# A macaron block on one core: router logits with the router as stationary operand, a new written-out order, and idle matmuls placed inside it

## What is computed

```python
x = x + 0.5 * ffn(layernorm(x))
x = x + attn(layernorm(x))          # 16 heads of 16, each query sees the last 64 keys
x = x + 0.5 * ffn(layernorm(x))

def ffn(X):                         # E = 8 routed experts, top K = 2, and a shared one; hidden 128
    shared = silu(X @ sW1 + sb1) @ sW2 + sb2
    logits = X @ routing_W.T + expert_bias
    activation = sqrt(softplus(logits))
    top_vals, top_idx = top_k(activation, 2)
    combine = sum(one_hot(top_idx, 8) * top_vals[..., None], axis=-2)
    y = silu(X @ rW1[e] + rb1[e]) @ rW2[e] + rb2[e]      # for every expert e
    return shared + einsum('ne,end->nd', combine, y)
```

## Time and profile before

| | us |
|---|---|
| median of 3 runs | 1542.52 (1542.23 to 1547.29) |
| profiled execution | 1542.9 |
| its span, first to last instruction | 1541.2 |
| PE busy in the span | 1496.8 (97%) |
| DVE, ACT, POOL busy | 1160.1, 1132.4, 803.4 |
| mean granted TensorE clock | 0.987 |

### The profile page before, as it was taken

How to read it: one execution, slowest core, us unless ns; L and a number is a source line. 1 busy time by engine, 2 the same in 40 slices (tenths; PEclk the granted TensorE clock), 3 DMA queues, 4 the chain that set the end, 5 groups by cost and what they waited for, 6 DMA issues and landing times.

```text
span 1541.2 us, 41196 instructions
## 1 busy us (share of the span) xinstructions
PE 1496.8 (97%) x13863; PEld 1350.0 (88%) x13863; DVE 1160.1 (75%) x4773; ACT 1132.4 (73%) x3416; POOL 803.4 (52%) x794
## 2 busy tenths in 40 slices
PE   8988999999999999999999999999999999999898
PEld 7887889888998889899898988989898898989787
DVE  6767777868788686877868788786877778686664
ACT  6467777778777777777778777777867778677753
POOL 4444555546455554645546465554645556354443
PEclk9999999999999999999999999999999999999799
DMA  3165536364363635536263453727335362534410
GB/s 119 39 183 149 156 103 194 83 179 132 95 174 111 186 98 152 145 101 183 97 173 119 130 140 117 193 76 193 118 113 156 121 176 84 161 101 133 119 54 28
DMA packets 264391, 199.65 MB, mean 130 GB/s; under 512 B 150859, under 2 KB 220918, under 8 KB 264182
## 3 DMA queue, kind: packets, MB, share of 16 engines
q1 hardware_dynamic: 263972, 196.94, 44.7%
q10 hardware_dynamic: 178, 0.02, 0.0%
q0 software_dynamic: 32, 0.07, 0.0%
HBM read 141.86 MB, written 42.43 MB: 120 GB/s over the span
## 4 chain that ended last, share of the span: by engine, by line
PE 73%; DVE 10%; issue 5%; SPq 4%; POOL 4%; DMA 2%; ACT 2%; DVEq 0%; POOLq 0%; ACTq 0%
PE gb L1069 10%; PE gb L1071 10%; PE gb L1070 9%; PE yb L1069 7%; PE yb L1070 7%; PE yb L1071 7%; PE ptb L1142 6%; PE sb_ L1133 5%; PE cxb L1161 3%; POOL gl L676 2%; PE gb L1183 2%; PE gb L1181 2%; DMA gate<-gates_pair 2%; DVE pr L938 2%; SPq L583 2%
## 5 line engine op out<-in xcount | busy, mean ns | idle before, releaser
L676 POOL TENSOR_TENSOR gl<-ag,gh 128x512 fp32r<-128x512 f32 x288 | 387.9, 1352 | 310.6 <-ACT gh L779 306.6
L732 ACT ACTIVATE pr<-pr,mx 128x128 f32<-128x128 f32 x1024 | 397.2, 392 | 35.1 <-DVE mx L938 31.5
L659 POOL TENSOR_TENSOR pr<-pr,rinv 128x512 f32<-128x512 f32 x256 | 278.3, 1094 | 233.2 <-DVE rinv L946 231.7
L1069 PE MATMUL yb<-w2h,gh 128*128 128x256 f32 x1152 | 334.9, 291 | 3.6 <-POOL gl L676 3.3
L1071 PE MATMUL yb<-w2l,gh 128*128 128x256 f32 x1152 | 322.6, 280 | 0.0
L1070 PE MATMUL yb<-w2h,gl 128*128 128x256 f32 x1152 | 322.5, 280 | 0.0
L938 DVE CUSTOM_DVE_ANT_0 pr<-sb_,mask 128x128 f32<-128x128 f32 x1024 | 236.0, 286 | 76.0 <-PE ptb L1142 48.8
L794 ACT ACTIVATE tt<-gb,b1half 128x512 f32<-128x512 f32 x288 | 195.9, 682 | 122.8 <-PE gb L1071 109.2
L1069 PE MATMUL gb<-xh,w1h 128*128 128x512 f32 x576 | 243.1, 422 | 2.3 <-DVE ag L1010 1.8
L779 ACT ACTIVATE gh<-ag 128x512 fp32r<-128x512 f32 x288 | 178.7, 626 | 83.6 <-DVE ag L1016 50.0
L1010 DVE SCALAR_TENSOR_TENSOR ag<-gb,b,gate 128x512 f32<-128x512 f32 x256 | 188.8, 745 | 65.7 <-ACT tt L794 33.4
(11 more groups left out here) (157 smaller groups left out, 2776.1 us busy)
## 6 DMA issues: line engine op xcount, KB each, us to landing
gate<-gates_pair SPq DMA_DIRECT2D x240, 256.0 KB, 3.9
ks<-qk_dram SPq DMA_DIRECT2D x256, 128.0 KB, 2.8
qs<-qk_dram SPq DMA_DIRECT2D x512, 64.0 KB, 2.5
...
```

Of the source, the lines that this page charges most:

```text
L659: nc.gpsimd.tensor_tensor(pr[:, k], pr[:, k], rinv[:, k, :].unsqueeze(2).to_broadcast([P, NP, P]), ALU.mult).then_inc(a_pn, 1)
L676: nc.gpsimd.tensor_tensor(gl[:, k, :], ag[:, k, :], gh[:, k, :].bitcast(F32), ALU.subtract).then_inc(f_gl, 1)
L732: nc.scalar.activation(pr[:, k, r, :], pr[:, k, r, :], ACT.Exp, bias=mx[:, k, r:r + 1], scale=-1.0, accum_out=rsum[:, k, r:r + 1]).then_in ...
L1069: nc.tensor.matmul(dst, ah, bh, start=start, stop=False, **kw)
```

## The change

**Logits.** The router becomes the stationary operand, padded with zeros to 128 columns (`rw` grows). `L` is four matmuls of 512 columns (two halves of the features, `xh` and `xl`), which give rounded-part logits on rows 0 to 7 and residue logits on rows 8 to 15. ACT copies the 128x512 result to SBUF (new step `lt`), and PE's new step `M` multiplies it, in four plain f32 matmuls of 8 columns, with a 0/1 matrix `fold` that both turns it back and adds the two parts. DVE then needs one addition where it had two.

**Constants.** POOL makes `fold` (a memset, two selects) and zeroes the pad of `rw` (a memset): `NCONST` goes from 19 to 23.

**Order.** All tables are written anew. New `Zg` steps are idle matmuls that write into the bank of the next step that takes one (so they wait for that bank). `ORDER` has two of them with two matmuls each (ahead of `P0` and of `pY1`, 36 matmuls in nine rounds), `HEAD` has 23, `TAIL` 60. Plain `Z` matmuls are 81 in `HEAD` and 16 in `TAIL`.

**Waits.** Three are added that the tables' order already implies (`aR` for `qT`, both halves of `ST` for the write of the scores' operands, the first experts' `a` for the weights' residues).

```diff
-qY8-7 S1-5 U15-6 V1-5 pY0-4 S2-5 O0-6 P0-5 S3-5 pH1-4 P1-5 S4-5 pH2-4 O1-6 S5-5 pH3-4 U1-5 pH4-4 pY1-4 P2-5
+V1-5 S1-5 qY8-7 S2-5 Zg2:P0-5 P0-5 pY0-4 O0-6 S3-5 O1-6 pH1-4 pH2-4 S4-5 pH3-4 pH4-4 P1-5 Zg2:pY1-4 pY1-4
+qX0-6 P2-5 U1-5 S5-5 qX1-6 pY2-4 P3-5 pH5-4 S6-5 qL-6 pH6-4 S7-5 pY3-4 qM-6 pY4-4 P4-5 U3-5 pY5-4 P5-5 pH7-4
...
-        rw = sb("rw", [P, KC, 2 * E], F32R)
+        rw = sb("rw", [P, KC, P], F32R)
+        fold = sb("fold", [P, E])
...
+            nc.gpsimd.memset(fold[:], 0.0).then_inc(w_const, 1)
+            nc.gpsimd.memset(rw[:, :, 2 * E:].bitcast(F32), 0.0).then_inc(w_const, 1)
...
+            select(fold[:], ALU.not_equal, 1.0, 0, [[-1, E]], 1)
+            select(fold[:], ALU.not_equal, 1.0, -E, [[-1, E]], 1)
...
+                elif s[1:] == "lt":
+                    n = nth(s, b)
+                    act.wait_ge(f_lgt, n + 1)
+                    nc.scalar.activation(lgt, bank(s[0] + "L", b), ACT.Copy).then_inc(f_lgs, 1)
...
-                acc = psum[:, 0:NT * 2 * E].rearrange("p (t e) -> p t e", t=NT)
-                op(nc.vector.tensor_tensor(lg[:], acc[:, :, E:2 * E], ebias[:].unsqueeze(1).to_broadcast([P, NT, E]),
-                                           ALU.add))
-                op(nc.vector.tensor_tensor(lg[:], acc[:, :, 0:E], lg[:], ALU.add))
+                op(nc.vector.tensor_tensor(lg[:], psum[:, 0:NT * E].rearrange("p (t e) -> p t e", t=NT),
+                                           ebias[:].unsqueeze(1).to_broadcast([P, NT, E]), ALU.add))
...
+                if s[:2] == "Zg":
+                    tile = take_bank(*users[next(ahead)])
+                    for _ in range(int(s[2:].split(":")[0])):
+                        nc.tensor.matmul(tile[:, 0:P], ident[:], ident[:], start=True, stop=True, skip_group_check=True)
...
-                    for t in range(NT):
-                        ts = slice(t * P, (t + 1) * P)
-                        for k in range(KC):
-                            nc.tensor.matmul(tile[:, 2 * E * t:2 * E * t + 2 * E], xh[:, q, k, ts], rw[:, k, :],
-                                             start=(k == 0), stop=False, skip_group_check=True)
-                            mm = nc.tensor.matmul(tile[:, 2 * E * t:2 * E * t + E], xl[:, q, k, ts], rw[:, k, 0:E],
-                                                  start=False, stop=(k == KC - 1), skip_group_check=True)
+                    for k in range(KC):
+                        nc.tensor.matmul(tile, rw[:, k, :], xh[:, q, k, :], start=(k == 0), stop=False)
+                        mm = nc.tensor.matmul(tile, rw[:, k, :], xl[:, q, k, :], start=False, stop=(k == KC - 1))
+                    mm.then_inc(f_lgt, 1)
+                elif s[1] == "M":
+                    n = nth(s, b)
+                    pe.wait_ge(f_lgs, n + 1)
+                    for t in range(NT):
+                        mm = nc.tensor.matmul(bank(s[0] + "L", b)[:, E * t:E * t + E], lgt[:, t * P:(t + 1) * P], fold[:],
+                                              start=True, stop=True, skip_group_check=True)
```

More of the change, by code:

```diff
@@ new lines @@
+pH6=1 P1=0 pH7=1 Z2=0 S4=0 pH8=1 P2=0 S5=0 pX0=2 U1=0 pX1=2 P3=0 S6=0 S7=0 pY6=1 P4=0 U3=0 pL=2 P5=0 S8=0
+pY7=1 P6=0 S9=0 pY8=1 P7=0 U5=0 S10=0 pM=2 pH0=2 U7=0 P8=0 Zg2=0 S11=0 Zg5=0 P9=0 Zg4=0 S12=0 aX0=1 P10=0
+aX1=1 U9=0 S13=0 Zg2=1 Q00=1 P11=0 Q01=1 S14=0 pC=2 U11=0 P12=0 S15=0 V0=1 Q10=1 Q11=1 P13=0 pY0=2 pH1=2
+U13=0 P14=0 pH2=2 pH3=2 P15=0 pH4=2 U15=0 pY1=2 V1=1 S0=1 O0=0 O1=0 S1=1 pY2=2 pY3=2 S2=1 pH5=2 S3=1 pH6=2
+P0=1 pH7=2 pY4=2 P1=1 S4=1 qX0=0 qX1=0 U1=1 P2=1 S5=1 pY5=2 qL=0 P3=1 S6=1 pH8=2 qM=0 qH0=0 U3=1 S7=1 P4=1
@@ new lines @@
+pH4=12 S5=11 qX0=10 P3=11 S6=11 pY1=12 qX1=10 pY2=12 pH5=12 S7=11 pH6=12 qL=10 pY3=12 qM=10 pY4=12 U3=11
+P4=11 pY5=12 pH7=12 pH8=12 qH0=10 P5=11 pY6=12 S8=11 P6=11 U5=11 qC=10 S9=11 pY7=12 P7=11 S10=11 pY8=12
+qH1=10 qH2=10 pX0=13 S11=11 U7=11 qY0=10 P8=11 qH3=10 pX1=13 qH4=10 qY1=10 P9=11 aX0=12 qY2=10 aX1=12 qH5=10
+qH6=10 P10=11 S12=11 pL=13 qY3=10 P11=11 Q00=12 pM=13 S13=11 U9=11 U11=11 qY4=10 S14=11 Q01=12 qH7=10 qH8=10
+P12=11 qY5=10 pH0=13 qY6=10 Q10=12 S15=11 V0=12 P13=11 qY7=10 qY8=10 U13=11 pC=13 P14=11 Q11=12 P15=11
@@ new lines @@
+pY0=13 U15=11 S0=12 V1=12 S1=12 Zg3=12 S2=12 O0=11 O1=11 P0=12 S3=12 pH1=13 P1=12 pH2=13 S4=12 pH3=13 U1=12
+P2=12 S5=12 pH4=13 S6=12 qX0=11 P3=12 pY1=13 qX1=11 S7=12 pY2=13 pH5=13 pH6=13 qL=11 pY3=13 qM=11 pY4=13
+U3=12 P4=12 pY5=13 pH7=13 P5=12 pH8=13 qH0=11 S8=12 P6=12 U5=12 pY6=13 qC=11 S9=12 pY7=13 P7=12 S10=12
+pY8=13 qH1=11 qH2=11 pX0=14 S11=12 U7=12 qY0=11 pX1=14 P8=12 qH3=11 qH4=11 qY1=11 P9=12 aX0=13 aX1=13 qY2=11
+P10=12 S12=12 qH5=11 P11=12 qY3=11 pL=14 Q00=13 S13=12 pM=14 U9=12 U11=12 qY4=11 Q01=13 S14=12 qH6=11 qH7=11
@@ new lines @@
+qH8=11 qY5=11 S15=12 P12=12 Q10=13 qY6=11 V0=13 P13=12 pC=14 Q11=13 U13=12 P14=12 pH0=14 qY7=11 P15=12
+qY8=11 S0=13 U15=12 V1=13 pY0=14 S1=13 O0=12 O1=12 S2=13 P0=13 Zg2=13 P1=13 pH1=14 S3=13 pH2=14 pH3=14 S4=13
+U1=13 P2=13 pH4=14 S5=13 P3=13 qX0=12 S6=13 pY1=14 pY2=14 qX1=12 S7=13 pH5=14 pH6=14 qL=12 pY3=14 qM=12
+pY4=14 U3=13 P4=13 pY5=14 pH7=14 pY6=14 pH8=14 qH0=12 P5=13 S8=13 qC=12 U5=13 P6=13 pY7=14 P7=13 S9=13
+qH1=12 pY8=14 S10=13 pX0=15 qH2=12 U7=13 qH3=12 qY0=12 S11=13 P8=13 qH4=12 pX1=15 S12=13 qY1=12 aX0=14 P9=13
@@ new lines @@
+qY2=12 aX1=14 qH5=12 S13=13 qY3=12 pL=15 P10=13 Q00=14 pM=15 P11=13 qY4=12 Q01=14 qH6=12 S14=13 qH7=12 U9=13
+U11=13 qY5=12 Q10=14 qH8=12 S15=13 qY6=12 pH0=15 P12=13 Q11=14 qY7=12 P13=13 pC=15 V0=14 qY8=12 P14=13
+U13=13 S0=14 P15=13 pY0=15 S1=14 U15=13 V1=14 S2=14 O0=13 P0=14 S3=14 O1=13 pH1=15 pH2=15 P1=14 S4=14 pH3=15
+P2=14 S5=14 pH4=15 U1=14 qX0=13 S6=14 P3=14 pY1=15 qX1=13 pY2=15 pH5=15 pH6=15 qL=13 pY3=15 qM=13 S7=14
+pY4=15 P4=14 pY5=15 pH7=15 P5=14 pH8=15 qH0=13 P6=14 pY6=15 S8=14 U3=14 U5=14 qC=13 S9=14 pY7=15 P7=14
@@ L459, in run @@
                 for s, off in words(ORDER[engine]):
-                    if 0 <= i + off < B and (s, i + off) not in apart_:
+                    if 0 <= i + off < B and (s[s.find(":") + 1:], i + off) not in apart_:
                         step(s, i + off)
@@ L500, in macaron_block @@
         run("PE", note)
+        ahead = iter(ahead)
         def bank(s, b):
```

382 lines of the change are left out of this document (183 added, 199 removed).

## The result

| | before | after |
|---|---|---|
| median | 1542.4 us (1538.3 to 1547.3, 4 runs) | 1619.1 us (1616.0 to 1624.9, 4 runs) |
| profiled span | 1541.2 | 1614.3 |
| mean granted clock | 0.987 | 0.987 |

The change makes the kernel 5% slower: ratio 1.050 (1.047 to 1.052). The forecast was 1541 us, in a range of 1527 to 1556.

The account below looks back on a forecast made before the run. PE was taken as the bound, with free time in head and tail. Logits +4.5, rounds +2, head 0 and tail -8 gave -1.5 us on the 1541.2 span, stated as 1541 us, range 1527 to 1556.

Parts of the forecast that it names:

- What bounds the kernel: Whole kernel: PE is the bound, 1496.8 of 1541.2 us busy; free time is in the head and above all the tail.
- Idle matmuls in the round: Repeating rounds: idles at P0 and pY1 partly fill waits; 0.9 us of planned waits replace 0.97 at C.
- The term for all rounds: Nine repeating rounds: waits and idle matmuls together cost +2 us, between -3 and +9.
- The logits on PE: L, M and an edge between unlike matmuls: 1.84 us against 1.70 a pass, +4.5 us in 32 passes.
- the doubt on f32: At M: if each of four FP32 passes needed its own load, 1.7 us, adding 27 us in all.
- rival 4: At L: long matmuls reusing weights overlap more, 0.13 us each, -12 us in all, 1529; chance 0.02.
- The logits elsewhere: ACT's copy adds 18.8 us, DVE loses 6.1; in the rounds costed at nothing, about 2 us where the router's result is awaited.
- The head: Before the rounds: first X up to 0.8 us later, against 20.8 us of PE idle time; 0, from -6 to +4.
- The tail: Last batches: idle matmuls keep the clock up and expert work moves behind the last O; -8 us, at best 13 gained.
- Rival 2: Each round and three like it in the tail gain a 1 us wait, at M or P0 and pY1; 1553; chance 0.19.
- rival 1: No new waits replace the old: rounds -3, head -6, tail -13, logits +3; 1524, or 1530; chance 0.28.
- Rival 3: In the tail the clock falls despite idles, or attention's chain sets the end: tail 0, 1549; chance 0.11.

Follow-up runs that it names:

- e2: Changed kernel with two SyncE steps, VS and OUT, moved behind the first four gate loads in all its tables: 1580.4 us, ratio 1.024.
- e5: e2 with the old logits (sixteen short matmuls at L; lt and M do nothing): 1586.5 us, ratio 1.032.
- e12: Changed kernel's new logits in every engine's order of the kernel before, without idle matmuls: 1652.6 us, ratio 1.073.
- e15: e12 with only lt and M put earlier, in the repeated rounds and the tail: 1604.7 us, ratio 1.040.
- e14: Changed code in the order of the kernel before, with the old logits and no idle matmuls: 1553.0 us, ratio 1.007.
- e8: Kernel before with 32 idle matmuls put into PE's waits in the attention of batch 15: 1538.8 us, ratio 0.9987.
- e4: Changed kernel with all 119 Zg idle matmuls left out: 1626.2 us, ratio 1.053.

## Why the prediction was wrong

**What bounds the kernel.** Right in that PE is the bound and that what it waits for is what counts. But it reads nothing of SyncE's queue. The step that failed is this one, under "Idle matmuls in the round": "So the new order has by its own plan 0.9 us of waits a round in exchange for the 0.97 at `C`." The term for all rounds was +2, with +9 as its upper end; the nine rounds measured +44.1, and the stretch up to the last attention, for which the sum has no term of its own, +18.8. The step looked at PE's table alone, at two places where idle matmuls had been put. SyncE's table was not costed at all, though the change puts `QW1` (1 MB) ahead of `pG1`, and `VS` (768 KB) ahead of the gates' loads. The trace of before could have shown the danger: DVE already waited 1.37 us for the gates in that round, and `H3` started 0.05 us behind the step that freed its bank. The price of `VS` and `OUT` ahead of the loads is 39 us (e2).

**The rounds without that.** e2's rounds are still 1.7 us longer than 91.2. The places: 0.54 ahead of `P0` and 0.94 ahead of `pY1`, the idles in them included; 0.42 ahead of `pY0`; 0.2 ahead of `pY2`; 0.54 ahead of the `S` behind `C`; two passes of the logits 0.2; less the 0.97 at the old `C`: 1.9 us, a little more than the 1.7. The trade was a loss, as the term of +2 had it, but its size was wrong: waits and idles of 2.7 us a round stand against the 0.97, and not 0.9. The longer way to the gates (`L`, `lt`, `M`) is not what costs here: with the old logits in the same order the rounds are no shorter (e5, 93.7), and the gates of `p` are copied earlier than before (those of `q`, counted from `S0`, 1.3 us later in e2). It costs where the order was not made for it (e12 to e15). How much of the new order's waits was needed to make room for it was not shown.

**The logits on PE.** Right, and a little dear. Rows of one pass, the start of `L` and of `M`, each with what stands behind it:

```profile
1563.41 0.39 PE L1205 MATMUL gb<-xh,rw 128*128 128x512 f32 x1
...
1564.34 0.39 PE L1089 MATMUL gb<-xh,w1h 128*128 128x512 f32 x1
...
1565.74 0.95 PE L1212 MATMUL gb<-fold,xn 128*128 128x8 f32 x8
1566.55 0.48 PE L1089 MATMUL gb<-xh,w1h 128*128 128x512 f32 x1
```

Here `L` is 0.93 us (forecast 0.91) and `M` 0.81 (0.85), together 1.74 where the old `L` took 1.70. That is the shortest of both. Over all 32 passes `L` takes 0.98 us on average and `M` 0.85, together 1.83, 0.09 more than the shortest, about the edge that was forecast at 0.08. The old `L` took 1.70 us in one kind of pass and 1.79 in the other, where a `P` follows it, on average 1.75 without one pass that stood in a wait. So it is +0.08 us a pass, +2.6 us in all, where the sum had +4.5. (By the prediction's own bounds the term's upper end is +5.4 us, not +7.) `M` stands as eight records for four matmuls, and costs 0.81 us and not 1.7, so the doubt on f32 fell as foreseen; rival 4 fell with the 0.23 us between the matmuls of `L`. For the 131 ns for N=512 that the Trainium skill gives in TensorE: Matmul & The Clock Gate, section Back-to-back issue gap, the trace still disagrees: the four of `L` are 0.23 us apart.

**The logits elsewhere.** "I cost this at nothing" held for the changed order: `M` doesn't appear in PE's waits there, VectorE waits 16.6 us in all for its result where it waited 17.1 for the old `L`, and e5 gains nothing by taking the detour out. The reasoning, by busy time on ACT and DVE and by a wait of `M` itself, would not have carried to another order: the gates come later by `lt` and `M`, and in the old order that costs 1.2 us a round at the best places tried (e15 against e14) and 6.3 at worse ones (e12).

**The head.** Forecast 0, measured +10.9. The first `X` moved by 0.9 us as worked out from the selects; that wait of PE is 6.2 us where it was 5.2. But `pX0` of batch 1 is 7.9 us later, so 7.0 us arise between the two. With the old logits in the new order (e5) `pX0` of batch 1 comes 2.1 us sooner, which fits the late first `lt` that the prediction read the earlier trace rows; the rest is the new head's own order, and `S0` of batch 2 is no earlier in e5 (250.5 us) than in e2 (249.8). In the old order with the changed code (e14) `S0` of batch 2 comes at 241.6. A better order that saves some of the 20.8 us of idle time was my hope, not a reading.

**The tail.** Forecast -8. The clock was right: 1.00 in the last attention, and that stretch is 8.8 us shorter. But the stretch behind it is 8.1 us longer, and the sum, 121.5 us, stands against 122.2. The prediction had the caution ("the moved work must still be done") and then priced it at too little: the shorter attention is work carried over. e8 shows the clock alone, with no work moved: about 2 us, not certainly there. In the changed kernel, dropping the idle matmuls makes the last attention 3.0 us longer (e4, 57.2 against 54.2).

**Rivals.** Rival 2 had the right side and the right rule: a wait in each round, decisive from 0.7 us on. Its places were not the main ones (beyond their idles, 0.1 us of wait stayed ahead of `P0` and 0.7 ahead of `pY1`), and the price of 12 us was far too low, since a third place was the bank of `H1`, freed by a step that waits for a DMA. Rivals 1 and 4 are out: waits took the place of the old ones, and the matmuls of `L` are no closer than 0.23 us. Rival 3 was right in part: the clock didn't fall, but the two last stretches together gave 0.7 us of the forecast 8. (In rival 1, half of the head's and the tail's gain makes 1533, not 1530.)

**The sum as it is now read**, from the profiled spans (73.1 us): SyncE's order 36.4 (1614.3 - 1577.9, e2). Then e2 against before: the head 12.3, the nine rounds 14.8, the next 9.1, the two last stretches together 0.5.

The medians of e5 and e14 split these last 38 us by kind. The changed code in the old order, with the old logits, costs about 10 us (e14, 1553.0). The new order of the engines with its idle matmuls, SyncE mended, adds 33.6 (e5, 1586.5). The new logits in place of the old then take 6.1 away (e2, 1580.4). So what is left beside SyncE's queue is mainly the new order itself. The split holds for this sequence of steps: in the old order the new logits cost 52 us (e15 against e14), 12 of them in the nine rounds. In the rounds the places are named above; which steps of the new head make it longer, beyond the first `X`, the first `lt` and a wait of 2.4 us for the gates at a `C`, and what makes up the 9.1 us of the next stretch, stays open.
